# A new steady order for every engine's queue, and the guard of the squared norms as a row-wise maximum

## The reference

```
xn = layernorm(x)
s  = mamba_block(xn)                 # 256 inner channels, 16 states, a scan over time
y  = xn
for i in range(6):                   # 6 layers
    y = attention(shift(y), Wqkv[i], q_scale[i], k_scale[i], Wo[i]) + y
    y = ffn(shift(y), ...) + y       # layernorm, gated GELU, inner size 341
out = x + s * silu(y)
```

```
l2norm(t) = t / max(||t||, 1e-12)
q = l2norm(q) * qs;  k = l2norm(k) * ksc
q = q * cos * scale + rotate_half(q) * sin * scale      # k likewise, with 1/scale
```

## Time and profile before

| | us |
|---|---|
| median of 3 runs (lowest, highest) | 1759.36 (1758.06, 1764.40) |
| the profiled execution, its own time | 1760.83 |
| its span, first to last instruction | 1758.8 |

### The profile page before, as it was taken

The page is one execution under the profiler, slowest core; times in us unless marked ns, Lnnn a source line. Parts: engine busy times, 40 slices in busy tenths (PEclk is TensorE's granted clock), DMA queues, the critical chain, the costliest instruction groups (busy, mean ns, idle before and its releaser), DMA issues.

```text
span 1758.8 us, 73907 instructions
## 1 busy us (share of the span) xinstructions
PE 1690.8 (96%) x30944; PEld 985.9 (56%) x30944; DVE 1526.9 (87%) x2751; ACT 1250.7 (71%) x2328; POOL 1405.4 (80%) x1264
## 2 busy tenths in 40 slices
PE   5899999999999999999999999999999999999987
PEld 2455555555555555555555555555555565555552
DVE  7688898989988999889988898898898989988966
ACT  4567687677776777866877668677777677786664
POOL 3576888878888887988889778897888888888872
PEclk9899999999999999999999999999999999999998
DMA  5113232132313322132321413314131242212240
GB/s 138 40 46 77 57 80 64 48 88 51 73 30 87 82 65 49 39 79 64 93 69 30 90 46 71 85 35 95 46 84 30 64 106 65 48 37 59 67 95 24
DMA packets 96694, 114.18 MB, mean 65 GB/s; under 512 B 42398, under 2 KB 62636, under 8 KB 96364
## 3 DMA queue, kind: packets, MB, share of 16 engines
q1 hardware_dynamic: 96364, 109.46, 26.2%
HBM read 19.22 MB, written 1.05 MB: 12 GB/s over the span
## 4 chain that ended last, share of the span: by engine, by line
PE 67%; DVE 14%; issue 7%; POOL 6%; ACT 3%; SPq 1%; DMA 1%; POOLq 0%; DVEq 0%; ACTq 0%
PE bank L709 13%; PE bank L734 9%; PE bank L793 9%; PE bank L725 7%; PE bank L810 6%; PE bank L754 5%; PE bank L771 4%; PE bank L838 3%; DVE qn L1486 3%; DVE qc L1486 3%; PE bank L853 2%; DVE ssq L1493 2%; PE bank L746 2%; PE bank L917 2%; POOL hb L1858 2%
## 5 line engine op out<-in xcount | busy, mean ns | idle before, releaser
L1813 POOL TENSOR_TENSOR AB<-qc,qn 128x512 f32<-128x512 f32 x384 | 487.1, 1274 | 123.6 <-DVE qn L1486 121.8
L1824 POOL TENSOR_TENSOR AB<-AB,rinv 128x512 f32<-128x512 f32 x384 | 391.3, 1042 | 31.0 <-DVE rinv L1511 30.9
L709 PE MATMUL bank<-wqkv,XT 128*128 128x512 f32 x768 | 381.9, 599 | 7.5 <-DVE qn L1486 5.6
L1831 POOL TENSOR_TENSOR Pb<-Pb,p_rden 128x512 f32<-128x512 f32 x192 | 200.4, 1044 | 150.1 <-DVE p_rden L1532 147.9
L1123 ACT ACTIVATE qkT<-bank 128x512 f32<-128x512 f32 x384 | 228.8, 596 | 108.8 <-PE bank L734 107.4
L1114 ACT ACTIVATE sq<-bank 128x512 f32<-128x512 f32 x384 | 228.3, 595 | 96.7 <-PE bank L709 94.7
L1486 DVE TENSOR_TENSOR qc<-bank,rt 128x512 f32<-128x512 f32 x384 | 258.6, 673 | 11.1 <-ACT sq L1114 9.4
L1493 DVE TENSOR_REDUCE ssq<-sq 128x8 f32<-128x512 f32 x384 | 258.5, 673 | 6.0 <-ACT sq L1114 5.3
L1486 DVE TENSOR_TENSOR qn<-bank,rt 128x512 f32<-128x512 f32 x384 | 261.6, 681 | 0.0
L734 PE MATMUL bank<-ident,AB 128*128 128x128 f32 x1536 | 244.7, 282 | 7.8 <-ACT qkT L1123 2.9
L793 PEld LDWEIGHTS bank<-PT,V 64*64 64x64 f32 x12288 | 198.5, 135 | 94.3 <-issue 89.5
(11 more groups left out here) (144 smaller groups left out, 2496.6 us busy)
## 6 DMA issues: line engine op xcount, KB each, us to landing
V<-V SPq DMA_DIRECT2D x672, 64.0 KB
rep<-du SPq DMA_DIRECT2D x64, 512.0 KB, 4.7
wqkv<-in_Wqkv SPq DMA_DIRECT2D x36, 256.0 KB, 3.4
XV<-XT SPq DMA_DIRECT2D x96, 64.0 KB, 2.1
wo<-in_Wo SPq DMA_DIRECT2D x6, 512.0 KB, 5.3
BC<-BC SPq DMA_DIRECT2D x8, 256.0 KB
w<-in_W SPq DMA_DIRECT2D x6, 341.0 KB, 4.6
xin<-in_x SPq DMA_DIRECT2D x4, 256.0 KB, 3.6
```

What stands on the lines that cost most here:

```text
L709: pe.matmul(R[u % 2][:], XT[:, s % NB, (u % 2) * P:(u % 2 + 1) * P], wqkv[:, (u // 2) * 512:(u // 2 + 1) * 512], start=True, stop=True).th ...
L1813: pool.tensor_tensor(AB[:, n % NAB, :], qc[:, u % 2, :], qn[:, u % 2, :], ALU.add).then_inc(rs_done, 1)
L1824: pool.tensor_tensor(o, o, r, ALU.mult).then_inc(nm_done, 1)
```

## The change

Three things change.

1. The guard. The buffer ssq, one number for each of 64 heads and halves, gets a second column that holds 1e-24 in every row and is set once at the start. The guard was a maximum with a constant (TENSOR_SCALAR, 64 elements in and out); it is now a maximum over rows of two (TENSOR_REDUCE, 128 elements in, 64 out).

2. The orders. The lists of the loop, the fill and part of the end are other permutations of the same calls on PE, ACT, DVE, POOL and SP. Some calls also change the iteration in which they stand (`turn(i, 0)` becomes `turn(i + 1, 0)` at the end of the list and moves into the fill for the first step), so that the cut of the loop lies elsewhere. The number of calls is the same, and so are all functions but the guard and the reduction that feeds it.

```
-        ssq = m.sb("ssq", [P, 64])
+        self.ssq = m.sb("ssq", [P, 64, 2])
+            pool.memset(k.ssq[:, :, 1], 1e-24).then_inc(made, 1)
...
-                dve.reduce_sum(ssq[:, 8 * u:8 * u + 8], sq[:, u % 2, :].rearrange("p (h d) -> p h d", d=DH), AX_X)\
+                dve.reduce_sum(ssq[:, 8 * u:8 * u + 8, 0], sq[:, u % 2, :].rearrange("p (h d) -> p h d", d=DH), AX_X)\
...
-                dve.tensor_scalar(ssc[:, q], ssq[:, q], 1e-24, None, ALU.max).then_inc(ssc_done, 1)
+                dve.reduce_max(ssc[:, q], ssq[:, q, :], AX_X).then_inc(ssc_done, 1)
```

3. On DVE, the part of the list around the guard (the end of a step):

```
                 softmax(i, 2)
                 rotate(i + 1, 5)
-                gate(i - 3, 0)
+                gate(i - 3, 1)
+                res_attention(i - 2)
+                sum_p(i, 2)
                 sum_squares(i + 1, 5)
-                sum_p(i, 2)
-                gate(i - 3, 1)
                 rotate(i + 1, 6)
                 gate(i - 3, 2)
-                res_attention(i - 2)
                 z_scan(i - 7, 11)
+                center(i - 2)
+                softmax(i, 3)
                 sum_squares(i + 1, 6)
-                softmax(i, 3)
-                center(i - 2)
                 sum_squares(i + 1, 7)
+                sum_p(i, 3)
                 guard_q(i + 1)
-                sum_p(i, 3)
                 z_scan(i - 3, 0)
                 rotate(i + 1, 7)
                 norm_q(i + 1)
```

More of the change, by code:

```diff
@@ L979, in _ @@
             turn(0, 7)
-            qk(1, 7)
+            qk(1, 5)
             scores(0, 3)
             turn_p(0, 2)
+            qk(1, 6)
+            values_out(0, 2)
+            qk(1, 7)
+            turn_p(0, 3)
             value(1, 0)
-            values_out(0, 2)
-            turn_p(0, 3)
+            values_out(0, 3)
+            turn(1, 0)
             value(1, 1)
-            for i in STEADY:
[L989 to L995, removed]
+            turn(1, 1)
+            value(1, 2)
+            scores(1, 0)
+            value(1, 3)
+            turn(1, 2)
+            for i in STEADY:
                 qk(i + 1, 0)
@@ L1668, in _ @@
             softmax(0, 1)
+            sum_squares(1, 1)
             rotate(1, 1)
[L1670 removed]
             sum_p(0, 1)
+            z_conv(0)
             rotate(1, 2)
             sum_squares(1, 2)
+            softmax(0, 2)
             rotate(1, 3)
             sum_squares(1, 3)
[L1676 removed]
+            sum_p(0, 2)
             rotate(1, 4)
+            softmax(0, 3)
             sum_squares(1, 4)
[L1679 removed]
             rotate(1, 5)
             sum_squares(1, 5)
[L1682 removed]
+            sum_p(0, 3)
             sum_squares(1, 6)
[L1684 removed]
             sum_squares(1, 7)
             guard_q(1)
[L1687 removed]
+            rotate(1, 6)
+            norm_q(1)
             rotate(1, 7)
[L1689 removed]
             for i in STEADY:
+                z_scan(i - 4, 1)
+                z_scan(i - 4, 2)
+                z_scan(i - 5, 4)
+                z_scan(i - 8, 12)
+                z_scan(i - 6, 6)
+                z_scan(i - 8, 13)
+                z_scan(i - 6, 7)
                 z_gate(i - 9)
                 res_ff(i - 4)
+                z_scan(i - 7, 10)
+                norm_x(i - 3)
                 softmax(i, 0)
[L1695 removed]
                 z_scan(i - 8, 14)
@@ new lines, in _ @@
+            normalise(1, 3)
+            normalise(1, 4)
+            normalise_p(1, 0)
+            rotate_sum(1, 7)
+            rotate_sum(2, 0)
+            normalise(1, 5)
+            normalise(1, 6)
+            rotate_sum(2, 1)
+            for i in STEADY:
+                z_bu(i - 4, 3)
+                rotate_sum(i + 1, 2)
+                z_bu(i - 5, 8)
+                z_hc(i - 8, 14)
+                normalise(i, 7)
+                z_hc(i - 6, 7)
+                z_bu(i - 7, 12)
+                z_bu(i - 3, 0)
+                z_hc(i - 4, 2)
+                normalise_p(i, 1)
+                z_hc(i - 7, 9)
+                rotate_sum(i + 1, 3)
+                z_bu(i - 4, 4)
+                z_bu(i - 3, 1)
+                z_bu(i - 7, 13)
+                z_delta(i - 2)
+                z_hc(i - 7, 10)
@@ new lines, in _ @@
+                z_bu(i - 6, 11)
+                z_hc(i - 3, 0)
+                z_hc(i - 4, 3)
+                normalise(i + 1, 2)
+                z_hc(i - 5, 6)
+                normalise(i + 1, 3)
+                normalise(i + 1, 4)
+                z_bu(i - 7, 15)
+                z_bu(i - 4, 7)
+                rotate_sum(i + 1, 7)
+                z_hc(i - 7, 12)
+                z_hc(i - 3, 1)
+                normalise_p(i + 1, 0)
+                rotate_sum(i + 2, 0)
+                normalise(i + 1, 5)
@@ L1965, in _ @@
+                z_hc(i - 7, 13)
+                normalise(i + 1, 6)
+                rotate_sum(i + 2, 1)
             normalise(LAST, 7)
```

328 lines of the change are left out of this document (144 added, 184 removed).

## The result

| | median us | ratio to before (95% interval) |
|---|---|---|
| before, 4 runs | 1759.95 | |
| changed, 4 runs | 1841.14 | 1.0458 (1.0443 to 1.0473) |

The change makes the kernel 81 us slower. The forecast was 1756, the range 1738 to 1777.

A forecast was written before the change was run, and what follows sets the result against it. PE, busy 98.6% of the steady stretch, was taken to set the pace; the terms summed to -3.3 us from the profiled 1760.83, giving 1757.5, or 1756.0 for the median, range 1738 to 1777.

The forecast's parts named there:

- rival of guess_v: ACT in even steps: guess_v ahead of copy_qk makes the second turn some 0.6 us late; 1776.4 us, chance 0.2.
- The lock on rinv: End of step 5 of six: POOL's z_bu no longer stands beside DVE's rinv and holds it; -2.2 us.
- the first turn_p: Step 5 of six on PE: a full-width matmul between scores and turn_p covers a 0.16 us wait; -1.3 us.
- The wait of var_x: Step 4 of six: PE's 0.93 us wait for square_x goes, but turn_p then waits for normalise_p; -1.2 us.
- fast rival: All the waits go, var_x's whole 0.93 us included, and the transition has no price; 1742.9 us, chance 0.33.
- The swap: PE: full-width matmuls put between scores and turn_p cost 0.05 us in each of 138 places; +4.6 us net.
- guess_v: ACT: guess_v directly ahead of the next step's first copy_qk makes turn 0.1 us late in eight steps; +0.8 us.
- The fill: Step 0: z_conv and copy_p change place with what they hold up, reducing PE's waits and low clock; -4 us.

The follow-up runs named there:

- forwarded kernel: Changed kernel with, on SP only, doublings 2 to 4 of BC moved forward between the V moves that follow the first doubling: 1740.78 us, ratio 0.9887.
- z_conv alone: Kernel before with one call moved: in the fill on DVE, z_conv(0) stands behind sum_p(0, 1), ACT as before: 1760.63 us, ratio 1.0004.

## Why the prediction was wrong

The step that failed is its first: "So PE sets the pace, and a new order can win only what PE waits, and lose by what it adds to PE." An order can also add waits, anywhere in a chain that reaches PE. The prediction adds one itself, on ACT, in its rival of guess_v. But the sum follows PE, DVE, ACT and POOL, and has no term for SP, whose list the change permutes as well: none of the 30 rows is of SP's queue, and no rival is. The chain through z_hc, SP, BC and z_bu was already at its limit: 27.9 us, with POOL waiting for BC at its end in four of seven batches, 0.9 to 1.5 us. These waits in the kernel before (us, times):

```profile
  issue: 5.0, 4
```

Both ends of that chain were moved. That is 98.9 us of waiting on POOL where the prediction has 0.

The other steps, from the changed and the forwarded kernel:

*The lock on rinv: right.* rinv is at 0.23 in all steady steps, the one of 1.20 is in step 0 (at 44.6 us), and the guard is never held (shortest, median, longest in ns; the earlier trace rows):

```profile
L1512 DVE TENSOR_REDUCE ssc<-ssq x49: 208/234/285, 34.9 to 1766.0; 128x64 f32<-128x128 f32 x47, 128x32 f32<-128x64 f32 x2
...
L1522 DVE SCALAR_TENSOR_TENSOR rinv<-tq,yq x49: 191/225/1195, 36.5 to 1767.6; 128x64 f32<-128x64 f32 x47, 128x32 f32<-128x32 f32 x2
```

Step 5 of six is 0.52 us shorter (34.24 to 33.72; 0.41 in the forwarded kernel), against 0.32 for the lock and 0.16 for the first turn_p. The guard itself is 0.234, forecast 0.27. Which of the two removed the lock is settled by the old guard in the forwarded kernel: rinv is free there too, so it was the order. That the guard is never held agrees with the Trainium skill (page "SBUF — State Buffer", section "Who interferes with whom"): a row reduction does not contend for the port shared with GpSimd on trn2; 285 ns at the longest here, against 766 before, and the old guard in the new order is held to 0.62 us.

*The wait of var_x: right.* It is gone, and turn_p waits in its place, 0.95 us (forwarded kernel; the earlier trace rows):

```profile
621.54 1.02 PE L832 MATMUL bank<-sqx,mean 128*128 128x512 f32 x2
624.75 0.63 PE L780 MATMUL bank<-ident,Pb 128*128 128x128 f32 x4 [0.95 <-POOL Pb L1842]
```

Step 4 of six gains 0.15 with the doublings forward (36.42 to 36.27), as forecast. The fast rival's 1742.9 lies near the forwarded kernel's 1740.8 by luck: its reason, the whole 0.93 back, did not come true.

*The swap: its price in a place is right, as a term of the sum it fails.* Forwarded kernel:

```profile
619.28 1.12 PE L718 MATMUL bank<-wqkv,XT 128*128 128x512 f32 x2
620.24 0.60 PE L780 MATMUL bank<-ident,Pb 128*128 128x128 f32 x4
620.68 0.59 PE L734 MATMUL bank<-wqkv,XV 128*128 128x512 f32 x1
```

Two matmuls behind scores take 0.96 us to the next group, against 0.86 without (614.49 to 615.35), +0.10, and what follows starts 0.44 later, not 0.49. But put back it costs 19.5 us, all of it PE waiting, and PE's busy time does not fall by the 6.9 of the term; taken alone into the kernel before it costs 37, half of it waiting, and PE's busy time rises by 15.5. So no single price holds for the swap. That the other engines are placed for it in each order fits the waits, and was not tried further.

*guess_v: no loss,* within the bound. In the forwarded kernel the second turn comes 1.07 us behind values_out as before (627.46 to 628.53; before 637.72 to 638.78).

*The fill: right in size, in part by the mechanism that was given.* Step 1 begins at 79.9 us (changed) and 78.5 (forwarded), against 84.3. In the changed kernel the low clock is gone, as forecast, and PE's wait for PT is 0.81, not 2.42; a wait for qn of 0.86 stands:

```profile
50.00:62.00 12.00, 9.64 (x232) 6.20 (x230) 11.63 (x24) 10.64 (x17) 5.68 (x5) 1.00 0.14 33
```
```profile
59.27 0.66 PE L745 MATMUL bank<-ident,AB 128*128 128x128 f32 x4 [0.81 <-ACT PT L1149]
```

z_conv alone brings none of it, by the experiment. The whole fill was reordered, copy_p with it, and which calls carry the gain was not tried.

With the doublings of BC together the change would be worth 19 us, where the terms of the sum gave 3.3. Of the forwarded kernel's gain 5.8 are in the fill and 2.6 behind the last step's start; of the rest, step 2 of six gives most (0.99 per six steps). In three such steps of before (8, 26 and 32) PE waits 3.8 us in all before scores, for nothing that the profile shows. Whether the order or chance removed these waits stays open.

## What to carry to other kernels

When a change permutes several queues, list for each shared buffer the chain that refills it (last reader, DMA queue, landing, first reader), and compare the time allowed with the time needed in the trace of before, the queue that only issues DMAs included. A chain of transfers that wait for one another belongs together in its queue: each V move put between two links, some 0.6 us of issue, makes the whole chain later. A bottleneck engine at 98.6% bounds what an order can win, never what it can lose.

## What the runs showed of the hardware that was not expected

After the wait of 10.9 us PE's granted clock is near the 1.2 GHz level (0.55 from 391.2 to 396.2 us; 1.00, the 2.4 GHz level, from there to 412.0), and two full-width matmuls take 1.92 us, not 1.02. The stretch, and one of PE's rows in it:

```profile
391.20:396.20 5.00, 4.95 (x15) 2.64 (x16) 1.70 (x3) 1.88 (x4) 3.59 (x3) 0.55 0.02 3
```
```profile
392.13 1.92 PE L720 MATMUL bank<-wqkv,XT 128*128 128x512 f32 x2
```

And the old guard, reading one column of the buffer with two, took 0.144 us in the middle (142 to 731 ns), where it took 0.196 on the dense buffer; the cause was not tried.
